# A selective-scan stage: diagonals by way of DRAM, and copies moved between VectorE and ScalarE

## The chip, the core and the metric

The kernel runs on one core of one Trainium2 chip. Its time is the device time of the whole program in microseconds (us). A core has a matrix engine (TensorE, "PE"; its weight loads are "PEld"), VectorE ("DVE"), ScalarE ("ACT"), GpSimd ("POOL") and SyncE ("SP", which here only issues transfers). The engines run side by side, each through its own instructions in program order, and wait for each other on counting semaphores.

## The reference, cut to what matters

The network is a convolutional state-space layer, then linear attention, then a spectral filter. The part at issue is the selective scan of the first layer. For each of 2 images and 4 directions `k` (rows, columns, and both backwards), with 256 channels, 16 states and 4096 positions:

```python
delta = softplus(dts + dt_proj_b)              # dts, B, C: projections of x
def step(h, inp):
    ut, dt, bt, ct = inp
    dA = exp(dt[..., None] * A)                # A = -exp(A_logs)
    h = dA * h + (dt * ut)[..., None] * bt     # one h for each channel and state
    y = einsum('bkdn,bkn->bkd', h, ct)
```

The four y are added in image order.

## The kernel before, in words

The program runs, for each image, a convolution, `scans`, and a norm with projection; then attention and the spectral filter for both. `scans` goes through 4 directions x 8 chunks of L = 512 positions, so 64 chunks in all. Channels lie on partitions in two halves t = 0, 1; positions lie along the free axis. Within a chunk (`body(c, nxt)`) all engines walk through the states n = 0..15:

- ScalarE: `decays(c, n, t)` (L617) makes exp(step x A). `times_b(c, n)` (L609) multiplies by B, which varies along positions: for even n it scales the turned x (position on partitions, `xu_tok`) into `scaled`; for odd n it scales the identity into four diagonal matrices `diag`. Both buffers are single, so `times_b(n)` waits until `drive(n-2)` is done (L605).
- PE: `drive(c, n)` (L508, L510) turns `scaled`, or multiplies `xu_tok` with `diag`, into `p_drive` in PSUM (two buffers, by the parity of n). It waits until scan n-2 has read the buffer. `sum_y` (L521) adds C x state into `p_y`.
- VectorE: `scan(c, n, t)` (L719) runs the recurrence over 512 positions; it needs `drive` and `decays` of that state and half. `state` is a ring of four.
- GpSimd: `times_c` (L663) multiplies the state by `c_wide`, and copies the last column to `carry` (L666), with which the next chunk starts.

While chunk c runs, the next one is prepared in the same loops: at n = 0 PE projects it (`project`), at n = 1 ScalarE copies that to `xd` (L582), at n = 3 and 4 PE makes the raw step of a half (`step_product`), at n = 4 and 5 VectorE takes its positive part (`step_bias`, L693, and L696 from the same function), at n = 6 and 7 ScalarE finishes the softplus (L593, L598), at n = 8 VectorE adds the two parts (`finish_step`, L701), GpSimd multiplies by u (`step_times_u`, L654), and PE turns the product (`turn_x`, L496, at n = 10 and 11), which VectorE copies to `xu_tok` (`keep_x`, L709). The y of the chunk before is copied from PSUM by VectorE after scan(3, 0) (`keep_y`, L726), turned back by PE and added by VectorE (`add_y`, L739). PE's order in a state n is: preparation, then `drive(n+2)`, then `sum_y(n-3)`. ScalarE's order is the loop

```python
for n in range(NS):
    of, at = following(c, nxt, n + 2)
    if of:
        decays(of, at, 0)
    of, at = following(c, nxt, n + 3)
    if of:
        times_b(of, at)
    of, at = following(c, nxt, n + 2)
    if of:
        decays(of, at, 1)
    if nxt and n in preparation:
        preparation[n](nxt)
```

and `decays(n, t)` waits for scan(n-2, t), for its buffer is double. SyncE stores the rows of C to DRAM (`store_c`) and loads them broadcast to all partitions, four states at a time (`widen_c`).

Of the kernel before, what the change touches and what calls it, by code (L numbers as in the profile page):

```python
# [9 lines left out]
fp32 = mybir.dt.float32  # L10
fp32r = mybir.dt.float32r
ALU = mybir.AluOpType
# [3 lines left out]
P = 128  # L16
# [7 lines left out]
NCH = T // L  # L24
START = 16
# [24 lines left out]
def constants(nc, m, io):  # L50


    with ExitStack() as ctx:
# [9 lines left out]
        w_conv = sb("w_conv", [P, 2, DT2, 9, P], fp32r)  # L63
        ps = [ctx.enter_context(nc.psum_tensor(f"wps{i}", [P, 512], fp32)) for i in range(8)]
# [30 lines left out]
        def _(pool):  # L95
# [12 lines left out]
                               pattern=[[4, 32], [0, 4]], channel_multiplier=-1).then_inc(made, 1)  # L108

# [89 lines left out]
def convolution(nc, m, io, b):  # L199


    with ExitStack() as ctx:
# [25 lines left out]
        def _(sp):  # L228
# [3 lines left out]
            sp.wait_ge(m.w_stored, 16)  # L232
# [121 lines left out]
    "projected", "xd_kept", "c_stored", "c_ready", "c_in0", "c_in1", "b_turned", "b_kept", "step_mm", "step_max",  # L354
# [38 lines left out]
def scans(nc, m, b):  # L393
# [3 lines left out]
    with ExitStack() as ctx:  # L397
        sb = lambda n, sh, d=fp32: ctx.enter_context(nc.sbuf_tensor(n, sh, d))
        ps = lambda n, sh: ctx.enter_context(nc.psum_tensor(n, sh, fp32))
        NB4 = L // P  # L400
# [7 lines left out]
        diag = sb("diag_b", [P, NB4, P])  # L408
# [24 lines left out]
        def _(sp):  # L433
            def store_c(c):
                sp.wait_ge(s["xd_kept"], START + c.g + 1)
                sp.dma_start(m.c_dram[c.parity], xd[C_ROW:C_ROW + NS, :]).then_inc(s["c_stored"], 16)
                sp.wait_ge(s["c_stored"], START + c.g * 16 + 16)
                sp.sem_inc(s["c_ready"], 1)
# [8 lines left out]
            def body(c, nxt):  # L447
                if c.first:
                    store_c(c)
                    widen_c(c, 0)  # L450
                    widen_c(c, 1)
# [10 lines left out]
        def _(pe):  # L462
# [37 lines left out]
            def drive(c, n):  # L500
                pe.wait_ge(s["scaled"], START + c.q + (n + 1))
                for t in range(DT2):
                    if not (c.first and n < 2):
                        pe.wait_ge(s["scanned"], START + c.q * 2 + (2 * n - 4 + t + 1))
                    for i in range(NB4):
# [3 lines left out]
                        else:  # L509
                            last = pe.matmul(o, xu_tok[:, c.parity, i, t * P:t * P + P], diag[:, i, :], start=True,  # L510
                                             stop=True)
# [64 lines left out]
        def _(act):  # L576
            def keep_projection(c):
# [3 lines left out]
                act.wait_ge(s["c_stored"], START + c.g * 16)  # L581
                act.copy(xd[:, :], p_prep[:, :]).then_inc(s["xd_kept"], 1)  # L582

            def keep_b(c):
                act.wait_ge(s["b_turned"], START + c.g + 1)
                rows = p_b[:, :].rearrange("p (i r) -> p i r", r=P)[:, :, B_ROW:B_ROW + NS]
                act.copy(b_tok[:, c.parity, :, :], rows).then_inc(s["b_kept"], 1)

# [11 lines left out]
            def times_b(c, n):  # L600
# [1343 lines left out]
```

## Time and profile before

| | |
|---|---|
| median of 3 runs | 6715.05 us (6708.61 to 6716.85) |
| the profiled execution | 6713.79 us, span 6712.1 us |
| busy, share of the span | PE 87%, PEld 77%, DVE 71%, ACT 52%, POOL 42% |
| mean granted TensorE clock | 0.954 |

A share is a mean over the whole span. The scans of the two images lie at about 180 to 1800 us and 2010 to 3640 us; from about 3700 us on the spectral filter runs, in which POOL is all but idle. A chunk is about 49 us, from one `finish_step` (L701) to the next.

### The profile page before, as it was taken

Reading aid. Unit: us, or ns where it says so; the run is one execution under the profiler, and the core shown is the slowest. Engines: PE = TensorE matmul, PEld = TensorE weight load, DVE = VectorE, ACT = ScalarE, POOL = GpSimd, SP = SyncE. Lnnn points to the kernel's source line nnn. Section 1 sums busy time; section 2 is a strip of 40 time slices with the busy share of each in tenths; the row PEclk is TensorE's granted clock in tenths of the full one; section 3 lists DMA queues with packets and bytes.
Section 4 is the critical chain, followed back from the end, with each engine's and each line's share of the span. In section 5 each row is a group of like instructions: output and inputs, shape, how many; then the busy total and the mean of one; then the engine's idle time right before and its main releaser. Section 6 shows DMA issues by size and latency. Waiting matters only on the chain. (4 is left out here: it accounts for less than half of the span.)

```text
span 6712.1 us, 130278 instructions
## 1 busy us (share of the span) xinstructions
PE 5830.3 (87%) x41691; PEld 5150.7 (77%) x41691; DVE 4764.7 (71%) x6882; ACT 3496.8 (52%) x7658; POOL 2798.1 (42%) x2159
## 2 busy tenths in 40 slices
PE   7789889898887998888888544999999989999998
PEld 6688778887766887888877333888888878888887
DVE  2799999999818999999997554555556556555554
ACT  2799999999737999999997211111111111111110
POOL 0688888888716888888887000000000000000000
PEclk8899999999988999999999877999999989999999
DMA  2122222222221222222222115666666667666665
GB/s 68 68 88 89 83 83 89 88 89 83 90 70 71 88 89 83 87 85 88 90 83 98 32 47 143 153 149 139 142 148 152 155 149 157 144 140 142 150 151 143
DMA packets 552406, 719.16 MB, mean 107 GB/s; under 512 B 37814, under 2 KB 458518, under 8 KB 518038
## 3 DMA queue, kind: packets, MB, share of 16 engines
q1 hardware_dynamic: 551382, 705.17, 38.6%
q10 hardware_dynamic: 720, 10.49, 0.4%
q8 instruction: 124, 2.03, 0.1%
q14 instruction: 180, 1.47, 0.1%
HBM read 677.22 MB, written 38.31 MB: 107 GB/s over the span
## 5 line engine op out<-in xcount | busy, mean ns | idle before, releaser
L663 POOL TENSOR_TENSOR read<-state,c_wide 128x1024 f32<-128x1024 f32 x1024 | 2435.0, 2378 | 459.2 <-DVE state L719 455.8
L719 DVE TENSOR_TENSOR_SCAN state<-decay,carry,p_drive 128x512 f32<-128x512 f32 x1792 | 2145.7, 1259 | 10.1 <-POOL carry L666 5.3
L617 ACT ACTIVATE decay<-step,a_neg 128x512 f32<-128x512 f32 x2048 | 1416.2, 714 | 230.2 <-DVE state L719 229.9
L1614 PE MATMUL p_y<-window,x_high 128*128 128x256 f32 x7936 | 1506.5, 288 | 0.0
L1677 ACT COPY term_blocks<-p_s 128x256 f32<-128x256 f32 x832 | 310.4, 373 | 2195.0 <-PE p_s L1614 2195.0
L1614 PEld LDWEIGHTS p_y<-window,x_high 128*128 128x128 f32 x7936 | 1253.9, 193 | 0.0
L510 PE MATMUL p_drive<-diag_b,xu_tok 128*128 128x128 f32 x8192 | 1101.3, 285 | 119.8 <-DVE state L719 116.1
L510 PEld LDWEIGHTS p_drive<-diag_b,xu_tok 128*128 128x128 f32 x8192 | 1007.8, 196 | 212.8 <-DVE state L719 151.2
L1614 PE MATMUL p_y<-window,x_low 128*128 128x256 f32 x3968 | 1138.8, 287 | 0.0
L521 PE MATMUL p_y<-ident,read 128*128 128x128 f32 x8192 | 1078.2, 275 | 3.8 <-POOL read L663 3.8
L521 PEld LDWEIGHTS p_y<-ident,read 128*128 128x128 f32 x8192 | 942.2, 143 | 4.7 <-POOL read L663 4.7
L609 ACT ACTIVATE scaled_x<-xu_tok,b_tok 128x256 f32<-128x256 f32 x2048 | 866.4, 494 | 44.7 <-DVE xu_tok L709 44.7
L1614 PEld LDWEIGHTS p_y<-window,x_low 128*128 128x128 f32 x3968 | 764.3, 193 | 0.0
L508 PE MATMUL p_drive<-ident,scaled_x 128*128 128x128 f32 x4096 | 574.8, 278 | 148.2 <-DVE state L719 136.4
L1614 PE MATMUL p_s<-window,x_high 128*128 128x256 f32 x2432 | 539.8, 310 | 148.3 <-DMA window<-taps_scratch 81.1
L508 PEld LDWEIGHTS p_drive<-ident,scaled_x 128*128 128x128 f32 x4096 | 462.3, 142 | 267.2 <-DVE state L719 175.0
L609 ACT ACTIVATE diag_b<-ident,b_tok 128x128 f32<-128x128 f32 x2048 | 648.6, 388 | 4.9 <-PE p_drive L510 4.5
L1614 PEld LDWEIGHTS p_s<-window,x_high 128*128 128x128 f32 x2432 | 390.2, 192 | 213.7 <-issue 118.7
L1734 DVE TENSOR_TENSOR term_blocks<-p_y,term_blocks 128x512 f32<-128x512 f32 x384 | 265.5, 692 | 354.2 <-PE p_y L1614 339.4
L1651 PE MATMUL p_mix<-term_blocks,mix_weights 128*128 128x512 f32 (+1 forms) x1280 | 461.2, 507 | 1.9 <-DVE term_blocks L1717 1.9
L1716 DVE TENSOR_TENSOR term_blocks<-p_y,term_blocks 128x256 f32<-128x256 f32 x448 | 187.7, 419 | 353.0 <-PE p_y L1614 352.1
L1651 PEld LDWEIGHTS p_mix<-term_blocks,mix_weights 128*128 128x128 f32 x1280 | 233.8, 190 | 152.0 <-issue 138.1
(245 smaller groups left out, 5822.3 us busy)
## 6 DMA issues: line engine op xcount, KB each, us to landing
c_wide<-c_scratch SPq DMA_DIRECT2D x256, 1024.0 KB, 4.6
window<-taps_scratch SPq DMA_DIRECT2D x448, 257.0 KB, 6.2
window<-taps_scratch SPq DMA_DIRECT2D x768, 129.0 KB, 4.6
window<-taps_scratch SPq DMA_DIRECT2D x192, 513.0 KB, 7.2
window<-taps_scratch SPq DMA_DIRECT2D x64, 385.0 KB, 5.9
gate_scratch<-gate_out SPq DMA_DIRECT2D x16, 512.0 KB, 3.1
gate_in<-gate_scratch SPq DMA_DIRECT2D x8, 1024.0 KB, 6.4
mix_weights<-in_M_plus SPq DMA_DIRECT2D x32, 256.0 KB, 7.2
```

Of the source, the lines that this page charges most:

```text
L508: last = pe.transpose(o, scaled[:, i, t * P:t * P + P], m.ident[:, :])
L510: last = pe.matmul(o, xu_tok[:, c.parity, i, t * P:t * P + P], diag[:, i, :], start=True, stop=True)
L521: last = pe.matmul(p_y[:, i, t * P:t * P + P], read[:, n % 4, t, i * P:i * P + P], m.ident[:, :], start=n == 0 and i % 2 == 0 and t == 0, ...
L609: last = act.activation(dst, src, ACT.Copy, scale=b_tok[:, c.parity, i, n:n + 1])
L617: act.activation(decay[:, n % 2, t, :], step[:, c.parity, t, :], ACT.Exp, scale=m.a_neg[:, DT2 * c.k + t, n:n + 1]).then_inc(s["decay"], 1)
L663: pool.tensor_tensor(read[:, n % 4, :, :], state[:, n % 4, :, :], wide, ALU.mult).then_inc(s["read_out"], 1)
L719: dve.tensor_tensor_scan(flip(state[:, n % 4, t, :], c), flip(decay[:, n % 2, t, :], c), flip(p_drive[:, n % 2, t, :], c), 0.0 if c.start ...
L1614: last = pe.matmul(out, x[:, source, blk, :], view[:, :, at:at + P][:, :, ::-1], start=first and x is m.x_high and z == 0, stop=True, skip ...
L1651: last = pe.matmul(p_mix[par][:, at:at + size], mix_now[:, kind, reach, :], filtered[:, j % 2, par ^ kind, kind, at:at + size], start=kind ...
L1677: act.copy(shared[:, i % 4, :, :], shared_bank(i)).then_inc(s["kept"], 1)
L1716: dve.tensor_tensor(to[:, :, 0:P], half_of(p_y[i % 4], 0), shared[:, i % 4, :, :], ALU.add)
L1734: dve.tensor_tensor(to.rearrange("p k (h t) -> p k h t", h=2), p_y[i % 4][:, :].rearrange("p (h k t) -> p k h t", h=2, k=2), out.rearrange ...
```

## The change

1. The diagonals of B for the 8 odd states are no longer made by ScalarE. SyncE writes the odd rows of B from `xd` into a zeroed DRAM scratch, each value to its place on a diagonal, and loads ready 128x128 matrices into `diag`, which now holds two groups of two odd states. The scratch is zeroed once at the start.
2. `keep_x` and `keep_y` become copies on ScalarE: at n = 10 and 11, and at the end of n = 3.
3. The positive part of the step becomes `step_max`, a Relu on ScalarE, at n = 4 and 5 between `times_b` and the second `decays`; VectorE keeps only `step_abs` there.
4. GpSimd copies the carries of two states at a time, after the odd one, and a scan of ring slot n waits for that pair.

```diff
@@ constants (sync) @@
+            sp.wait_ge(idmade, 4)
+            for parity in range(2):
+                sp.dma_start(m.diag_dram[parity].rearrange("(r x) -> r x", r=P), blank[:, :]).then_inc(m.w_stored, 16)
             sp.wait_ge(copied, 14)
@@ scans @@
-        diag = sb("diag_b", [P, NB4, P])
+        diag = sb("diag_b", [P, 2, 2, NB4, P])
@@ sync @@
-            def store_c(c):
+            def store_rows(c):
                 sp.wait_ge(s["xd_kept"], START + c.g + 1)
                 sp.dma_start(m.c_dram[c.parity], xd[C_ROW:C_ROW + NS, :]).then_inc(s["c_stored"], 16)
-                sp.wait_ge(s["c_stored"], START + c.g * 16 + 16)
-                sp.sem_inc(s["c_ready"], 1)
+                image = m.diag_dram[c.parity]
+                diagonals = bass.AP(tensor=image.tensor, offset=image.offset,
+                                    ap=[[NB4 * P * P, ODD], [P * P, NB4], [P + 1, P]])
+                rows = xd[B_ROW + 1:B_ROW + NS:2, :].rearrange("n (i p) -> n i p", p=P)
+                with nc.allow_non_contiguous_dma(reason="one value to each place of a diagonal"):
+                    sp.dma_start(diagonals, rows).then_inc(s["c_stored"], 16)
+
+            def load_diag(c, d):
+
+                if not (c.first and d < 2):
+                    sp.wait_ge(s["driven"], START + c.q * 2 + (8 * d - 8))
+                at = 2 * d * NB4 * P * P
+                src = m.diag_dram[c.parity, at:at + 2 * NB4 * P * P].rearrange("(n p q) -> p n q", n=2 * NB4, p=P)
+                sp.dma_start(diag[:, d % 2, :, :, :].rearrange("p n i q -> p (n i) q"), src).then_inc(
+                    s[f"diag_in{d % 2}"], 16)
...
+                load_diag(c, 2)
+                if nxt:
+                    store_rows(nxt)
                 widen_c(c, 2)
+                load_diag(c, 3)
                 widen_c(c, 3)
                 if nxt:
-                    store_c(nxt)
+                    sp.wait_ge(s["c_stored"], START + nxt.g * 32 + 32)
+                    load_diag(nxt, 0)
                     widen_c(nxt, 0)
+                    load_diag(nxt, 1)
                     widen_c(nxt, 1)
@@ tensor: drive @@
-                pe.wait_ge(s["scaled"], START + c.q + (n + 1))
+                if n % 2 == 0:
+                    pe.wait_ge(s["scaled"], START + c.g * ODD + (n // 2 + 1))
+                elif n % 4 == 1:
+                    pe.wait_ge(s[f"diag_in{n // 4 % 2}"], START + c.g * 32 + (16 * (n // 8) + 16))
@@ scalar @@
+            def step_max(c, t):
+                act.wait_ge(s["step_mm"], START + c.g * 2 + (t + 1))
...
+                act.activation(step[:, c.parity, t, :], p_prep[:, :], ACT.Relu, bias=bias).then_inc(s["step_max"], 1)
...
                 for i in range(NB4):
-                    dst, src = ((scaled[:, i, :], xu_tok[:, c.parity, i, :]) if n % 2 == 0 else
-                                (diag[:, i, :], m.ident[:, :]))
-                    last = act.activation(dst, src, ACT.Copy, scale=b_tok[:, c.parity, i, n:n + 1])
+                    last = act.activation(scaled[:, i, :], xu_tok[:, c.parity, i, :], ACT.Copy,
+                                          scale=b_tok[:, c.parity, i, n:n + 1])
...
+            def keep_y(c):
+                act.wait_ge(s["summed"], START + c.q + NS)
+                act.wait_ge(s["y_turned"], START + c.g * 2)
+                act.copy(y_tok[:, :, :], p_y[:, :, :]).then_inc(s["y_kept"], 1)
...
-                    if of:
+                    if of and at % 2 == 0:
                         times_b(of, at)
+                    if nxt and n in (4, 5):
+                        step_max(nxt, n - 4)
                     of, at = following(c, nxt, n + 2)
                     if of:
                         decays(of, at, 1)
+                    if n == 3 and not c.first:
+                        keep_y(Before(c))
                     if nxt and n in preparation:
                         preparation[n](nxt)
+                    if nxt and n in (10, 11):
+                        keep_x(nxt, n - 10)
@@ gpsimd @@
-                pool.tensor_copy(carry[:, n, :], state[:, n % 4, :, end]).then_inc(s["carried"], 1)
+                if n % 2:
+                    pool.tensor_copy(carry[:, n - 1:n + 1, :], state[:, n % 4 - 1:n % 4 + 1, :, end]).then_inc(s["carried"], 1)
@@ vector @@
-            def step_bias(c, t):
+            def step_abs(c, t):
+                dve.wait_ge(s["step_max"], START + c.g * 2 + (t + 1))
...
-                dve.tensor_scalar(step[:, c.parity, t, :], p_prep[:, :], bias, 0.0, ALU.add,
-                                  ALU.max).then_inc(s["step_max"], 1)
-                dve.wait_ge(s["step_max"], START + c.g * 2 + (t + 1))
                 dve.scalar_tensor_tensor(softplus[:, t, :], step[:, c.parity, t, :], -2.0, p_prep[:, :], ALU.mult,
                                          ALU.add).then_inc(s["step_abs"], 1)
...
-                        dve.wait_ge(s["carried"], START + c.q + (n - 3))
+                        dve.wait_ge(s["carried"], START + c.g * ODD + (n // 2 - 1))
...
                 for n in range(NS):
                     scan(c, n, 0)
-                    if n == 3 and not c.first:
-                        keep_y(Before(c))
                     if n in (6, 7) and not c.first:
                         add_y(Before(c), n - 6)
                     if nxt and n in (4, 5):
-                        step_bias(nxt, n - 4)
+                        step_abs(nxt, n - 4)
                     if nxt and n == 8:
                         finish_step(nxt)
-                    if nxt and n in (11, 12):
-                        keep_x(nxt, n - 11)
                     scan(c, n, 1)
```

## Rows read from the trace of the kernel before

**Rows 1.** Windows by stage; columns: engines' busy us, granted clock, DMA share, GB/s.

```profile
300.00:1500.00 1200.00, 1075.39 (x8479) 968.33 (x8480) 1108.04 (x1024) 1108.05 (x2460) 1030.11 (x804) 0.99 0.23 87
...
3700.00:6712.00 3012.00, 2622.06 (x17944) 2332.23 (x17944) 1698.70 (x4027) 414.50 (x974) 0.84 (x5) 0.94 0.59 136
```

**Rows 2.** Timeline of VectorE, one chunk: start, duration, what, idle before.

```profile
891.71 1.39 DVE L701 TENSOR_TENSOR step<-step,shared 128x1024 f32<-128x1024 f32 x1 [1.05 <-ACT shared L598]
...
903.65 16.50 DVE L719 TENSOR_TENSOR_SCAN state<-decay,carry,p_drive 128x512 f32<-128x512 f32 x14
922.05 1.23 DVE L726 COPY y_tok<-p_y 128x1024 f32<-128x1024 f32 x1 [1.90 <-PE p_y L521]
...
926.31 0.69 DVE L696 SCALAR_TENSOR_TENSOR shared<-step,p_prep 128x512 f32<-128x512 f32 x1
...
930.04 0.69 DVE L696 SCALAR_TENSOR_TENSOR shared<-step,p_prep 128x512 f32<-128x512 f32 x1
930.65 2.44 DVE L719 TENSOR_TENSOR_SCAN state<-decay,carry,p_drive 128x512 f32<-128x512 f32 x2
...
941.26 1.40 DVE L701 TENSOR_TENSOR step<-step,shared 128x1024 f32<-128x1024 f32 x1 [1.04 <-ACT shared L598]
```

**Rows 3.** Timeline of PE over the same chunk.

```profile
899.41 0.66 PE L496 MATMUL p_prep<-ident,shared 128*128 128x128 f32 x4 [0.69 <-POOL shared L654]
...
920.00 1.04 PE L508 MATMUL p_drive<-ident,scaled_x 128*128 128x128 f32 x8
920.87 1.04 PE L521 MATMUL p_y<-ident,read 128*128 128x128 f32 x8
```

**Rows 4.** Timeline of ScalarE over the same chunk.

```profile
922.89 1.69 ACT L609 ACTIVATE scaled_x<-xu_tok,b_tok 128x256 f32<-128x256 f32 x4
924.50 0.72 ACT L617 ACTIVATE decay<-step,a_neg 128x512 f32<-128x512 f32 x1
```

**Rows 5.** Timeline of GpSimd over the same chunk.

```profile
896.84 0.20 POOL L666 COPY carry<-state 128x2 f32<-128x2 f32 x1
896.98 2.37 POOL L654 TENSOR_TENSOR shared<-step,s 128x1024 f32<-128x1024 f32 x1
```

**Rows 6.** Groups, 180 to 3640 us: busy us, mean ns, idle before.

```profile
L663 POOL TENSOR_TENSOR read<-state,c_wide 128x1024 f32<-128x1024 f32 x1024 | 2435.0, 2378 | 459.2 <-DVE state L719 455.8 <-PE p_y L521 3.0
...
L617 ACT ACTIVATE decay<-step,a_neg 128x512 f32<-128x512 f32 x2048 | 1416.2, 714 | 230.2 <-DVE state L719 229.9
...
L609 ACT ACTIVATE scaled_x<-xu_tok,b_tok 128x256 f32<-128x256 f32 x2048 | 866.4, 494 | 44.7 <-DVE xu_tok L709 44.7
L609 ACT ACTIVATE diag_b<-ident,b_tok 128x128 f32<-128x128 f32 x2048 | 648.6, 388 | 4.9 <-PE p_drive L510 4.5
...
L693 DVE TENSOR_SCALAR step<-p_prep,dt_b 128x512 f32<-128x512 f32 x128 | 93.0, 727 | 261.1 <-PE p_prep L485 261.1
...
L709 DVE COPY xu_tok<-p_prep 128x512 f32<-128x512 f32 x128 | 86.9, 679 | 24.7 <-PE p_prep L496 23.9 <-ACT diag_b L609 0.8
L593 ACT ACTIVATE shared<-shared,dt_b 128x512 f32<-128x512 f32 x128 | 84.6, 709 | 14.1 <-DVE shared L696 14.1
...
L726 DVE COPY y_tok<-p_y 128x1024 f32<-128x1024 f32 x64 | 78.4, 1225 | 122.5 <-PE p_y L521 122.5
...
L582 ACT COPY xd<-p_prep 128x512 f32<-128x512 f32 x64 | 36.2, 566 | 5.9 <-PE p_prep L467 5.9
```

**Rows 7.** Timeline of SyncE at the start.

```profile
26.82 0.34 SPq L91 DMA_DIRECT2D w_conv_scratch<-w_conv  x1
```

**Rows 8.** Timeline of ScalarE, two places before the scans.

```profile
9.94 0.31 ACT L113 ACTIVATE a_neg<-a_neg 128x128 f32<-128x128 f32 x1 [7.84 <-DMA b_qkv<-in_attn_b]
...
181.61 1.28 ACT L620 ACT_TABLE_LOAD   x1 [3.78 <-PEq L202]
```

**Rows 9.** DMA issues: count, KB each, median us to landing.

```profile
c_wide<-c_scratch SPq DMA_DIRECT2D x256, 1024.0 KB, 4.6
...
c_scratch<-xd SPq DMA_DIRECT2D x64, 32.0 KB, 4.3
```

More of the change, by code:

```diff
@@ L24 @@
 NCH = T // L
+NB4 = L // P
+ODD = NS // 2
 START = 16
@@ L108, in _ @@
                                pattern=[[4, 32], [0, 4]], channel_multiplier=-1).then_inc(made, 1)
+            pool.memset(blank[:, :], 0.0).then_inc(idmade, 1)
         @block.scalar
@@ L509, in drive @@
                         else:
-                            last = pe.matmul(o, xu_tok[:, c.parity, i, t * P:t * P + P], diag[:, i, :], start=True,
-                                             stop=True)
+                            last = pe.matmul(o, xu_tok[:, c.parity, i, t * P:t * P + P],
+                                             diag[:, n // 4 % 2, n // 2 % 2, i, :], start=True, stop=True)
                     last.then_inc(s["driven"], 1)
@@ L587, in keep_b @@
                 act.copy(b_tok[:, c.parity, :, :], rows).then_inc(s["b_kept"], 1)
+            def step_max(c, t):
+                act.wait_ge(s["step_mm"], START + c.g * 2 + (t + 1))
+                if t == 0 and not c.first:
+                    act.wait_ge(s["decay"], START + c.q * 2 + -2 * NS)
+                bias = m.dt_b[:, DT2 * c.k + t:DT2 * c.k + t + 1]
+                act.activation(step[:, c.parity, t, :], p_prep[:, :], ACT.Relu, bias=bias).then_inc(s["step_max"], 1)
             def step_exp(c):
@@ L618, in decays, with keep_x @@
                                scale=m.a_neg[:, DT2 * c.k + t, n:n + 1]).then_inc(s["decay"], 1)
+            def keep_x(c, half):
+                act.wait_ge(s["x_turned"], START + c.g * 2 + (half + 1))
+                if not c.first:
+                    act.wait_ge(s["scaled"], START + c.g * ODD + -ODD)
+                    act.wait_ge(s["driven"], START + c.q * 2 + -2 * NS)
+                act.copy(xu_tok[:, c.parity, 2 * half:2 * half + 2, :],
+                         p_prep[:, :].rearrange("p (i d) -> p i d", d=DI)).then_inc(s["x_kept"], 1)
+            def keep_y(c):
+                act.wait_ge(s["summed"], START + c.q + NS)
+                act.wait_ge(s["y_turned"], START + c.g * 2)
+                act.copy(y_tok[:, :, :], p_y[:, :, :]).then_inc(s["y_kept"], 1)
             act.preload_act_table_set("natural_log_exp_and_others")
@@ L626, in body @@
                     keep_b(c)
+                    step_max(c, 0)
+                    step_max(c, 1)
                     step_exp(c)
                     step_ln(c)
-                    for n in range(2):
-                        times_b(c, n)
+                    keep_x(c, 0)
+                    keep_x(c, 1)
+                    times_b(c, 0)
                     for n in range(2):
@@ L644, in body @@
                         decays(of, at, 1)
+                    if n == 3 and not c.first:
+                        keep_y(Before(c))
                     if nxt and n in preparation:
                         preparation[n](nxt)
+                    if nxt and n in (10, 11):
+                        keep_x(nxt, n - 10)
+                if c.last:
+                    keep_y(c)
             chunk_stream(act, b, body)
@@ L684, in begin_y @@
                                          ALU.mult, ALU.add).then_inc(s["y_begun"], 1)
-            def step_bias(c, t):
-                dve.wait_ge(s["step_mm"], START + c.g * 2 + (t + 1))
+            def step_abs(c, t):
+                dve.wait_ge(s["step_max"], START + c.g * 2 + (t + 1))
                 if t == 0:
                     dve.wait_ge(s["x_turned"], START + c.g * 2)
-                    if not c.first:
-                        dve.wait_ge(s["decay"], START + c.q * 2 + -2 * NS)
-                bias = m.dt_b[:, DT2 * c.k + t:DT2 * c.k + t + 1]
-                dve.tensor_scalar(step[:, c.parity, t, :], p_prep[:, :], bias, 0.0, ALU.add,
-                                  ALU.max).then_inc(s["step_max"], 1)
-                dve.wait_ge(s["step_max"], START + c.g * 2 + (t + 1))
                 dve.scalar_tensor_tensor(softplus[:, t, :], step[:, c.parity, t, :], -2.0, p_prep[:, :], ALU.mult,
@@ L742, in body @@
                 if c.first:
-                    step_bias(c, 0)
-                    step_bias(c, 1)
+                    step_abs(c, 0)
+                    step_abs(c, 1)
                     begin_y(0)
```

28 lines of the change are left out of this document (9 added, 19 removed).

## The prediction

> **What bounds the kernel now.** I read the stages first [rows 1]: in a stretch of scans PE, VectorE, ScalarE and GpSimd are all busy for 1030 to 1108 of 1200 us, while the spectral stage is 3012 us that the change does not touch. So only some 3250 us of scans are at stake, in 64 chunks, and there no engine is far ahead of the rest: what matters is which wait ends last. The shares of the whole span hide that.
>
> Next I took one ordinary chunk, from `finish_step` at 891.71 to the next at 941.26, 49.55 us [rows 2], and looked at each engine in it. VectorE runs 14 scans in 16.50 us, 1.18 each, and after scan(3, 0) waits 1.90 us for PE's last sum before `keep_y`. Why is PE late? It starts `turn_x` at 899.41 after waiting for GpSimd's product, and from there has no idle row until `drive(4)` at 920.00 and the sum behind it at 920.87 [rows 3]. So from n = 10 to n = 3 PE sets the pace; VectorE, with its two x copies, only fits beside it. From `keep_y` to the next `finish_step` it is VectorE's turn: its operations follow each other, and PE, GpSimd and ScalarE wait for scans. That ScalarE does is seen in the groups: the decays wait 229.9 us, all for scans [rows 6]. The chunk is thus a loop of two parts, and each has to be priced by itself.
>
> **The change part by part.** *x copies.* VectorE gives up 128 copies of 679 ns [rows 6]. They lie in the part that PE paces, so I price the gain at nothing; without that cover it would be 2 x 0.6 x 64 = 77 us. *Diagonals on ScalarE.* 2048 activations of 388 ns go [rows 6], 648.6 us of busy time, but they were not what anyone waited for in either part, save that ScalarE's backlog vanishes: it reached `times_b(6)` at 922.89 [rows 4], though `drive(4)` was over at 920.00 + 1.04 = 921.04. PE's odd drives are the same matmuls. *Carries.* The product by u started 0.14 us after the carry before it [rows 5]. With n = 8 no longer copied it and the whole PE part come 0.15 us earlier. The pair makes an even scan wait for GpSimd's state n-3 instead of n-4. GpSimd needs at most 2.378 a state [rows 6] plus 0.14 a pair, 4.9, against 4.72 for four scans; nearly a tie, and the PE part covers it.
>
> *The second part, from `drive(4)` on,* is where the sign is decided. Before, `drive(4)` starts at 920.00 and scan(5, 1) at 930.65 [rows 2, 3], 10.65 us. Now it holds ScalarE's in-order list, so I write it out. An operation costs its mean less the 0.08 by which the next overlaps it (924.50 against 922.89 + 1.69 [rows 4]), except where another engine waits for its end. Prices [rows 6]: a decay 0.63; `times_b` 1.61; Relu with a bias column as the exponential with one, 0.71 (L593; a plain copy of that size, L582, is 0.57 and is the lower bound); the y copy 0.99, from the copy of 512 (0.566) and 0.106 for each further 128 elements (0.494 less 0.388), so 0.91 to the next start.
>
> - `drive(4)` starts at 919.85, ends at 920.9. ScalarE, with keep_projection behind it, is there about 921.0: `times_b(6)` to 922.6, second decay of state 5 to 923.25, `keep_y` (the sum is done by 921.8) to 924.15, first decay of state 6 to 924.8, `step_max` to 925.5.
> - Meanwhile scan(4, 0) has ended before 923, and VectorE stands at `step_abs(0)` until 925.55. It takes 0.61 (930.65 less 930.04 [rows 2]), so scan(4, 1) starts at 926.15. Before, `step_abs(0)` started at 926.31 [rows 2], so its scan at 926.92: 0.8 us gained here.
> - scan(4, 1) and scan(5, 0) end at 926.15 + 2.44 = 928.6. Only then may ScalarE start the decay of state 7 (it reads the buffer's release from scan(5, 0)): to 929.25, then `times_b(8)`, which stands ahead of `step_max(1)` because 5 + 3 is even: to 930.85, then Relu to 931.55. `step_abs(1)` from 931.6, scan(5, 1) at 932.2 against 930.65.
>
> So VectorE is spared 1.14 for y and twice 0.76, and stands still some 3 us at each of two places instead: net 1.5 us a chunk later. From scan(5, 1) on all is as before: the softplus is reached after the decays of state 8, so the wait of 1.04 before `finish_step` stays [rows 2]. Queued behind ScalarE's `keep_y` are just those decays and the Relu; PE's `sum_y(0)` waits for it too, but PE has the next `step_product` and `drive(5)` first. Behind VectorE's wait stands every scan.
>
> Bounds: with both Relus at 0.57, their ends overlapped and ScalarE free at 920.9, 0.9 a chunk; with ScalarE's backlog or the carry pairs adding 0.4, 1.9. Sixty chunks have both neighbours: 60 x 1.5 = 90 us (54 to 114). First and last chunks of an image have only one of the two parts; a few us either way, taken as 0.
>
> *The DRAM way.* 4096 values of 4 bytes are written and 2 MB of matrices loaded each chunk. The stretch of scans uses 0.23 of the DMA engines [rows 1]; a load of 1024 KB lands in 4.6 us, so four of 512 KB in at most that each, and the store of C in 4.3 [rows 9]. Scattered stores of single values are not in the trace. Nearest is the start: thirteen weight loads, several of single values, have landed by 9.94 us [rows 8]. I bound the store by 4.3 us below and 20 above (twice the whole start). It is issued about two states before `keep_y`, near 917, and its matrices are needed for `drive(1)`, some seven states after the next `finish_step`, near 958: less 5 for the load there are 36 us of cover, so it costs nothing. The C rows queued behind it on SyncE's queue have four states' notice, and `times_c` now waits only for scans (L663 [rows 6]). If cover failed, each us beyond would cost 60.
>
> The Trainium skill (DMA: Bandwidth & Descriptors, Rules for kernel authors) says that a non-contiguous last dimension becomes one descriptor per element, and (Why a DMA increments its semaphore by 16 and not by 1) that the slowest dimension limits the engines used; here it is 8, so this store would take 8 of 16 engines. No row here shows that; by it the store is slower than one spread over 16, which leaves the sum alone unless 36 us are passed.
>
> *Start.* 4 MB of zeros are stored before the w_conv store at 26.82 [rows 7]. Queued behind the loads that landed at 9.94 [rows 8] at 4.6 us a MB they end near 28.3, so 0 to 2 us. First chunks: `store_rows` is covered by the long additions of y.
>
> The Relu on ScalarE costs 0.71 where VectorE took 0.727 [rows 6], about equal by itself. The Trainium skill (ScalarE: Activation LUTs, Rules for kernel authors) says to use VectorE, not ScalarE, for relu. The trace agrees with no large difference in duration; it is the place in the list that hurts, which that rule does not price.
>
> The profiled execution took 6713.8, 1.3 below the median. 6713.8 + 90 + 1 = 6805. A difference within 0.2% (13 us) can hardly be told from none.
>
> **The rivals.**
>
> *VectorE relieved (faster), 0.18.* If ScalarE answered in time, the y copy with its wait (1.90 + 1.14) and two Relus (1.52) would go, 4.55 a chunk, less about 1.1 because `step_product(0)` comes only after the sum: 3.4 x 60 = 205, 6510. For it: VectorE is the busiest in the scans with ScalarE [rows 1], and 258 us of its busy time go [rows 6]. Against: the written order. It decides where `drive(4)` to scan(5, 1) takes under 10.8 us; I have 12.3. An in-between, PE reaching `drive(4)` a us or two sooner, gives 6650 to 6700.
>
> *A draw, 0.05:* the gain at `step_abs(0)` is larger (the sum earlier, copies shorter) and meets the loss at `step_abs(1)`. 6715.
>
> *The scattered store is late, 0.05:* at 50 us instead of under 36, each chunk is 14 longer: 7550. For it: its price is unknown. It then shows as PE waiting for a DMA before an odd `drive`.
>
> *Relu needs its table, 0.02:* a load takes 1.28 us [rows 8]; two Relus between exponentials need four, 5.1 us a chunk, 7020 or more. Against: copy, exponential and logarithm already alternate without a load.
>
> **How the numbers follow.** The likeliest case, 0.70, is slower by 50 to 120 us: its own range is 6765 to 6835, its centre 6805. With the draw that is 0.75; reaching down to 6650 takes in the mild third of the faster case, 0.05 to 0.06, and up to 6850 an overshoot of my own. Slower 0.70 + 0.05 + 0.02 = 0.77, same 0.05, faster 0.18.
>
> **What would show it.** In the chunk's timeline after: VectorE idle 2.5 to 3 us before each of the two `step_abs`, released by ScalarE's Relu; no idle before the y copy's old place; 12.3 us from `drive(4)` to scan(5, 1); a chunk of some 51 us; VectorE's busy time 258 us less and its share lower, not higher. ScalarE's rows in order: decay, `times_b`, Relu. I am wrong if those two waits are under 2 us each, if `drive(4)` lies well before 28 us after `finish_step`, or if PE waits for a matrix load.

## The result and the profile after

The changed kernel takes 6788.58 us (median of four runs, 6785.8 to 6799.3) against 6714.93 before on the same chip (6708.61 to 6716.85): ratio 1.0111, interval 1.0094 to 1.0127. The change makes the kernel slower by 1.1%, some 74 us. The forecast was 6805 us, with a range of 6650 to 6850.

The page of the changed kernel, head and busy time:

```profile
span 6788.2 us, 128900 instructions
...
PE 5829.7 (86%) x41691; PEld 5188.8 (76%) x41691; DVE 4552.1 (67%) x6562; ACT 3123.5 (46%) x5930; POOL 2735.6 (40%) x1648
```

The window that answers to [rows 1], a stretch in the scans (engines' busy us with counts, in the order PE, weight loads, VectorE, ScalarE, GpSimd; then granted clock, DMA share, GB/s):

```profile
300.00:1500.00 1200.00, 1047.61 (x8273) 955.67 (x8271) 1002.09 (x880) 942.99 (x1763) 980.51 (x595) 0.97 0.48 126
```

Every engine is less busy in the same 1200 us and none has become the bound: they wait for each other more. The DMA engines' share has doubled, from 0.23 to 0.48, with the matrices and the scattered store. Who waits is in the groups from 180 to 3700 us (busy us, mean ns, idle before and its releasers); VectorE:

```profile
L753 DVE SCALAR_TENSOR_TENSOR shared<-step,p_prep 128x512 f32<-128x512 f32 x128 | 88.0, 688 | 644.5 <-ACT step L626 644.5
L758 DVE TENSOR_TENSOR step<-step,shared 128x1024 f32<-128x1024 f32 x64 | 82.4, 1288 | 87.3 <-ACT shared L637 87.3
```

ScalarE:

```profile
L655 ACT ACTIVATE decay<-step,a_neg 128x512 f32<-128x512 f32 x2044 | 1422.0, 717 | 600.1 <-DVE state L768 589.1
L646 ACT ACTIVATE scaled_x<-xu_tok,b_tok 128x256 f32<-128x256 f32 x2048 | 867.5, 495 | 53.9 <-PE p_drive L540 53.6
L626 ACT ACTIVATE step<-p_prep,dt_b 128x512 f32<-128x512 f32 x128 | 85.8, 671 | 9.5 <-PE p_prep L514 9.5
...
L663 ACT COPY xu_tok<-p_prep 128x512 f32<-128x512 f32 x128 | 73.9, 577 | 78.9 <-PE p_prep L525 78.9
...
L669 ACT COPY y_tok<-p_y 128x1024 f32<-128x1024 f32 x63 | 62.5, 993 | 8.1 <-PE p_y L553 8.1
```

`step_abs` (L753) waits 644.5 us for ScalarE's Relu. Two waits, 256.6 of these, stand at the first chunk of each image, where 256.3 of the 261.1 before L693 in [rows 6] stood too; the other 388 are new. ScalarE itself is idle more than before, 600.1 us against 230.2 ahead of the decays, and nearly all of it for VectorE's scans. The two engines wait for each other in turn; neither is short of time.

One ordinary chunk shows it. VectorE, from one `finish_step` (L758) to the next, answering to [rows 2]:

```profile
913.54 1.39 DVE L758 TENSOR_TENSOR step<-step,shared 128x1024 f32<-128x1024 f32 x1 [1.05 <-ACT shared L637]
914.86 8.30 DVE L768 TENSOR_TENSOR_SCAN state<-decay,carry,p_drive 128x512 f32<-128x512 f32 x7
923.53 14.39 DVE L768 TENSOR_TENSOR_SCAN state<-decay,carry,p_drive 128x512 f32<-128x512 f32 x12 [0.38 <-POOL carry L729]
938.48 5.97 DVE L768 TENSOR_TENSOR_SCAN state<-decay,carry,p_drive 128x512 f32<-128x512 f32 x5 [0.56 <-PE p_drive L540]
947.81 0.69 DVE L753 SCALAR_TENSOR_TENSOR shared<-step,p_prep 128x512 f32<-128x512 f32 x1 [3.36 <-ACT step L626]
948.41 2.44 DVE L768 TENSOR_TENSOR_SCAN state<-decay,carry,p_drive 128x512 f32<-128x512 f32 x2
953.82 0.69 DVE L753 SCALAR_TENSOR_TENSOR shared<-step,p_prep 128x512 f32<-128x512 f32 x1 [2.96 <-ACT step L626]
954.43 2.45 DVE L768 TENSOR_TENSOR_SCAN state<-decay,carry,p_drive 128x512 f32<-128x512 f32 x2
...
965.04 1.41 DVE L758 TENSOR_TENSOR step<-step,shared 128x1024 f32<-128x1024 f32 x1 [1.04 <-ACT shared L637]
```

ScalarE between `drive(4)` and the second Relu of that chunk:

```profile
943.29 1.70 ACT L646 ACTIVATE scaled_x<-xu_tok,b_tok 128x256 f32<-128x256 f32 x4
944.88 0.71 ACT L655 ACTIVATE decay<-step,a_neg 128x512 f32<-128x512 f32 x1
945.50 0.99 ACT L669 COPY y_tok<-p_y 128x1024 f32<-128x1024 f32 x1
946.39 0.73 ACT L655 ACTIVATE decay<-step,a_neg 128x512 f32<-128x512 f32 x1
947.01 0.67 ACT L626 ACTIVATE step<-p_prep,dt_b 128x512 f32<-128x512 f32 x1
949.72 0.72 ACT L655 ACTIVATE decay<-step,a_neg 128x512 f32<-128x512 f32 x1 [2.04 <-DVE state L768]
950.89 0.72 ACT L655 ACTIVATE decay<-step,a_neg 128x512 f32<-128x512 f32 x1 [0.45 <-DVE state L768]
951.52 1.69 ACT L646 ACTIVATE scaled_x<-xu_tok,b_tok 128x256 f32<-128x256 f32 x4
953.12 0.67 ACT L626 ACTIVATE step<-p_prep,dt_b 128x512 f32<-128x512 f32 x1
```

and PE's `drive(4)`, from whose start the forecast counts the second part:

```profile
942.08 1.04 PE L540 MATMUL p_drive<-ident,scaled_x 128*128 128x128 f32 x8
```

The wait of 2.96 us is made by VectorE itself: it stands at `step_abs` for a Relu that stands behind a decay (950.89) that had to wait for VectorE's scan. The list adds 0.72 + 1.69 + 0.67 before it lets VectorE go. Over the 62 intervals of the table below the two waits are 3.19 and 2.97 us on the mean; before, both were 0.03.

Over all 62 intervals from one `finish_step` to the next inside an image, mean start times behind `finish_step`, in us (my tabulation of the two timelines):

| | `turn_x` | `drive(4)` | first `step_abs` | second `step_abs` | next `finish_step` |
|---|---|---|---|---|---|
| before | 8.01 | 28.40 | 34.67 | 38.39 | 49.29 |
| after | 7.87 | 27.95 | 33.68 | 39.69 | 50.62 |

A chunk is 1.33 us longer: 62 x 1.33 = 82 us. The first `finish_step` is 2.1 later (203.7 to 205.9), the gap between the images 1.6 shorter, and all that follows the last `finish_step`, nearly only stages that the change does not touch, 6.4 shorter: 76 in all, as the spans have it (6788.2 less 6712.1). These last three differences are no larger than the scatter between the profiles: in those of the experiments the first `finish_step` lies between 200.7 and 205.4 us, and what follows the last takes 3141 to 3170.

The matrices come in time (count, KB each, median us to landing, answering to [rows 9]):

```profile
c_wide<-c_scratch SPq DMA_DIRECT2D x256, 1024.0 KB, 4.8
diag_b<-diag_scratch SPq DMA_DIRECT2D x256, 512.0 KB, 4.0
```

PE has no wait for a DMA in any group of the scans.

### The profile page after: what moved, and what is told of

It is laid out like the page before. It is cut to its first block and busy times, and to the rows that moved or that the text cites. A ratio compares the mean times of both kernels' runs of the same rounds, so it can differ in the third digit from the quotient of the medians.

```text
span 6788.2 us, 128900 instructions
## 1 busy us (share of the span) xinstructions
PE 5829.7 (86%) x41691; PEld 5188.8 (76%) x41691; DVE 4552.1 (67%) x6562; ACT 3123.5 (46%) x5930; POOL 2735.6 (40%) x1648
## 2 busy tenths in 40 slices
DMA packets 1081526, 858.12 MB, mean 126 GB/s; under 512 B 304598, under 2 KB 987446, under 8 KB 1046966
## 5 line engine op out<-in xcount | busy, mean ns | idle before, releaser
L542 PE MATMUL p_drive<-diag_b,xu_tok 128*128 128x128 f32 x8192 | 1087.7, 286 | 200.6 <-DVE state L768 200.6
L553 PE MATMUL p_y<-ident,read 128*128 128x128 f32 x8192 | 1097.8, 279 | 6.9 <-POOL read L725 3.7
L553 PEld LDWEIGHTS p_y<-ident,read 128*128 128x128 f32 x8192 | 962.6, 145 | 8.2 <-POOL read L725 8.2
L540 PEld LDWEIGHTS p_drive<-ident,scaled_x 128*128 128x128 f32 x4096 | 477.9, 145 | 227.1 <-DVE state L768 142.0
L753 DVE SCALAR_TENSOR_TENSOR shared<-step,p_prep 128x512 f32<-128x512 f32 x128 | 88.0, 688 | 644.5 <-ACT step L626 644.5
```

What stands on the lines that cost most here:

```text
L540: last = pe.transpose(o, scaled[:, i, t * P:t * P + P], m.ident[:, :])
L553: last = pe.matmul(p_y[:, i, t * P:t * P + P], read[:, n % 4, t, i * P:i * P + P], m.ident[:, :], start=n == 0 and i % 2 == 0 and t == 0, ...
```

## The experiments

Times are medians; a ratio is to the kernel before, run on the same chip. A difference in us is worked out from a ratio: its distance from 1, times 6715. Chips differ by some us (the kernel before took 6708 to 6733), so an expected time is compared with 6715 times the ratio.

**1. The changed kernel with the positive part back on VectorE.** The rest of the change stays.

```
-                dve.wait_ge(s["step_max"], START + c.g * 2 + (t + 1))
+                dve.wait_ge(s["step_mm"], START + c.g * 2 + (t + 1))
...
+                dve.tensor_scalar(step[:, c.parity, t, :], p_prep[:, :], bias, 0.0, ALU.add,
+                                  ALU.max).then_inc(s["step_max"], 1)
```

> The changed kernel with one part undone: the positive part of the step is again made by VectorE, in front of step_abs. Theory (the loss is the Relu behind other work in ScalarE's list): in the changed kernel's chunk VectorE would start scan(4, 1) near 946.45 instead of 948.41 and scan(5, 1) near 950.3 instead of 954.43, so about 4.2 us a chunk less than the changed kernel, 6788.6 - 62 x 4.2 = 6530 (6490 to 6600), well faster than before; VectorE's idle time before step_abs falls from 644 us to under 300. Rival (the diagonals' transfers, or the pair copies of the carries, cost the time): it stays at 6715 or above.

6567.85 us, ratio 0.9762 (0.9744 to 0.978), inside what was expected. A chunk falls to 46.81. The Relu's move alone decides the sign: with it 1.1% slower, without it 2.4% faster, 234 us apart.

**2. The changed kernel with the Relu at the head of its state in ScalarE's list,** ahead of the decays and `times_b`; same engine, same instruction.

```
                 for n in range(NS):
+                    if nxt and n in (4, 5):
+                        step_max(nxt, n - 4)
                     of, at = following(c, nxt, n + 2)
```

> The changed kernel with step_max moved to the head of its state in ScalarE's list, ahead of both decays and of times_b; nothing else differs. Theory (the place in the list): the second Relu is ready when scan(5, 0) ends, scan(5, 1) starts near 950.85 instead of 954.43, 3.6 us a chunk: 6788.6 - 62 x 3.6 = 6565 (6520 to 6640). Rival (ScalarE is the wrong engine for a Relu whatever its place, or handing over between engines costs the time): no more than 1 us a chunk, 6725 or above.

6601.42 us, ratio 0.9806 (0.9787 to 0.9825). The second wait is all but gone and the first shorter (0.20 and 2.63 us on the mean):

```profile
946.53 0.69 DVE L753 SCALAR_TENSOR_TENSOR shared<-step,p_prep 128x512 f32<-128x512 f32 x1 [2.52 <-ACT step L626]
947.13 2.44 DVE L768 TENSOR_TENSOR_SCAN state<-decay,carry,p_drive 128x512 f32<-128x512 f32 x2
949.77 0.69 DVE L753 SCALAR_TENSOR_TENSOR shared<-step,p_prep 128x512 f32<-128x512 f32 x1 [0.20 <-ACT step L626]
```

So 0.0305 of the ratio, 205 of the 234 us, goes with the place in the list, the engine being the same. That is the step on which the forecast's sign stood.

**3. The Relu alone moved to ScalarE,** in the kernel before.

> The kernel before with one part done: the positive part of the step as a Relu on ScalarE at the place that the change gives it. Here times_b is there for odd states too, so it stands ahead of both Relus. Theory: step_abs(0) starts about 1.9 us later than before and step_abs(1) another 2.2, 4.1 us a chunk: 6715 + 62 x 4.1 = 6970 (6900 to 7020). Rival (the Relu costs nothing by itself, the loss comes from the other parts): within 20 us of 6715.

7029.53 us, ratio 1.0444 (1.0423 to 1.0465): 298 us slower, in the upper end of what was expected (7013 by the ratio), and a chunk is 54.15. VectorE has its y copy with the wait for the sum, and the two waits for the Relu besides:

```profile
937.23 1.23 DVE L731 COPY y_tok<-p_y 128x1024 f32<-128x1024 f32 x1 [2.00 <-PE p_y L521]
938.37 2.44 DVE L724 TENSOR_TENSOR_SCAN state<-decay,carry,p_drive 128x512 f32<-128x512 f32 x2
943.43 0.69 DVE L701 SCALAR_TENSOR_TENSOR shared<-step,p_prep 128x512 f32<-128x512 f32 x1 [2.62 <-ACT step L594]
944.03 2.44 DVE L724 TENSOR_TENSOR_SCAN state<-decay,carry,p_drive 128x512 f32<-128x512 f32 x2
949.43 0.69 DVE L701 SCALAR_TENSOR_TENSOR shared<-step,p_prep 128x512 f32<-128x512 f32 x1 [2.96 <-ACT step L594]
```

The mechanism is the same; together with the other parts of the change it costs less.

**4. The y copy alone on ScalarE.**

```
-                dve.tensor_copy(y_tok[:, :, :], p_y[:, :, :]).then_inc(s["y_kept"], 1)
+                act.copy(y_tok[:, :, :], p_y[:, :, :]).then_inc(s["y_kept"], 1)
```

> The kernel before with one part done: the copy of y on ScalarE at the end of n = 3. Theory (the y copy is where the change gains): scan(5, 1) starts about 1.2 us sooner, then ScalarE's odd times_b make up the rest: 6715 - 74 = 6640 (6600 to 6690). Rival (the y copy on ScalarE delays decays and costs as well): 6715 or above.

6701.9 us, ratio 0.9956 (0.994 to 0.9972): 30 us gained, where some 75 were expected. VectorE no longer waits for the sum, but for the raw step (`step_product`), which PE makes behind it. The profile names a decay before the first of the two, but PE ends the first raw step at 917.83:

```profile
918.19 0.75 DVE L702 TENSOR_SCALAR step<-p_prep,dt_b 128x512 f32<-128x512 f32 x1 [0.82 <-ACT decay L617]
...
923.37 0.75 DVE L702 TENSOR_SCALAR step<-p_prep,dt_b 128x512 f32<-128x512 f32 x1 [1.35 <-PE p_prep L485]
```

The group before `step_bias` is idle 393.4 us against 261.1 in [rows 6], 132 in 62 intervals or 2.1 a chunk, and PE's sums wait 69.2 us for the later `y_tok`. Of the 3.1 us freed (1.90 + 1.23 [rows 2]) most went there.

**5 to 7. The other parts alone,** in the kernel before: the diagonals by way of DRAM; the two x copies on ScalarE; one carry copy for two states.

> The kernel before with one part done: the diagonals of B by way of DRAM, all else as before (positive part, x copies and y copy on VectorE, a carry copy for each state). Theory (the transfers lie under 36 us of cover, and ScalarE's diagonals were not waited for, save a backlog of some tenths): PE reaches drive(4) up to 0.3 us a chunk sooner, 6715 - 19, so 0 to 30 us less than the kernel before on this chip. Rival (the transfers contend with the engines or come late): 13 us or more above it.

> The kernel before with one part done: the two x copies of a chunk on ScalarE. Theory (they lie in the part of the chunk that PE paces, where VectorE has slack): no gain from VectorE's 1.3 us a chunk; ScalarE, which here still makes the odd diagonals, gets 1.0 us a chunk more in that part, so 0 to 40 us above the kernel before. Rival (VectorE's load sets the time of this part): 1.2 us a chunk less, about 75 us below it.

> The kernel before with one part done: the carries copied in pairs. Theory (nearly a tie, covered by PE; only the copy at n = 8 shortens the way to PE's turn_x by 0.14 us): 0 to 10 us below the kernel before. Rival (the scan's wait for a younger state costs): VectorE's idle time before even scans of 0.4 us and more a chunk reaches PE's drives, 25 us or more above it.

The diagonals: 6751.98, ratio 1.0032 (1.0022 to 1.0043), 21 us slower where a draw or a small gain was expected: a miss. The x copies: 6771.91, 1.006 (1.0046 to 1.0073), 40 slower, the upper end of what was expected. The pairs: 6722.97, 0.9989 (0.998 to 0.9998), 7 faster, as expected.

Why do the x copies cost 40 us alone? Their groups on VectorE:

```profile
L723 DVE TENSOR_TENSOR_SCAN state<-decay,carry,p_drive 128x512 f32<-128x512 f32 x1792 | 2164.4, 1262 | 84.7 <-ACT decay L617 39.5 <-PE p_drive L508 29.0 <-PE p_drive L510 9.9
L723 DVE TENSOR_TENSOR_SCAN state<-decay,p_drive 128x512 f32<-128x512 f32 x256 | 295.1, 1202 | 36.0 <-ACT decay L617 28.6 <-PE p_drive L508 5.4 <-PE p_drive L510 1.6
```

The scans wait 68.1 us for decays, against 8.0 in the kernel before. From `turn_x` to `drive(4)` a chunk takes 20.97 us and not 20.39. With `times_b` for all sixteen states, ScalarE seems to have no room for two copies between n = 10 and n = 3.

**8. The best kernel: experiment 1 with the logarithm directly behind the exponential,** at n = 6 and not 7.

```
-            preparation = {1: keep_projection, 6: step_exp, 7: step_ln, 9: keep_b}
+            preparation = {1: keep_projection, 6: lambda c: (step_exp(c), step_ln(c)), 9: keep_b}
```

> The version with the positive part on VectorE again (6568 us), and ScalarE's logarithm directly behind its exponentials at n = 6, ahead of times_b for state 10. Theory (the second part of a chunk is VectorE's chain, and the wait of 1.05 us before finish_step is all ScalarE's order): that wait goes, 62 x 1.05 = 65 less: 6503 (6490 to 6530). Rival (PE or GpSimd sets the chunk by now): no more than 20 us less, 6548 or above.

6546.91 us, ratio 0.9727 (0.9712 to 0.9742): faster than both kernels, but only some 23 us under experiment 1, where 65 were expected: a miss. `finish_step` no longer waits for ScalarE; it takes twice as long instead. VectorE, then GpSimd over the same stretch:

```profile
943.57 2.53 DVE L760 TENSOR_TENSOR step<-step,shared 128x1024 f32<-128x1024 f32 x1
```

```profile
942.65 2.37 POOL L721 TENSOR_TENSOR read<-state,c_wide 128x1024 f32<-128x1024 f32 x1 [1.18 <-DVE state L770]
944.96 1.18 POOL L725 COPY carry<-state 128x4 f32<-128x4 f32 x1
```

GpSimd's product ends at 945.02. `finish_step`, 1.29 us long in the changed kernel's group, ends at 946.10, 1.1 behind that, as if it had begun only then; and GpSimd's carry, 0.20 elsewhere, ends at 946.14, at the same time as it. In all 62 intervals inside an image `finish_step` starts before the product's end and ends 1.08 or 1.09 us behind it. From experiment 1 to this one, 64 `finish_step` go from 1298 to 2525 ns, 79 us, and the 88.9 us of waiting before them, which went, are thus nearly all paid back. The Trainium skill (SBUF — State Buffer, SBUF: two separate sides) says that a VectorE operation with two inputs in SBUF and a GpSimd operation that reads SBUF exclude each other, and whoever comes second is fully held up. `finish_step` has two such inputs, and the trace agrees, in both directions. What was expected of this run did not reckon with it.

**9. All but the diagonals:** the four other parts together, while ScalarE still makes the diagonals.

> The whole change except its first part: the kernel before with the positive part, the copy of summed y and the copies of turned x on ScalarE and the carries in pairs, while ScalarE still makes the diagonals of B for the odd states. If the parts simply add up, the time is that of the kernel before plus what each of the four did alone (297 for the positive part, -30 for y, +40 for x, -7 for the pairs), about 300 more: 7015 (6960 to 7070), and the diagonals by way of DRAM, which cost 21 alone, are worth some 225 in company. If ScalarE's list can't be shortened by the DRAM way at the places that matter, the four parts together cost little more than the whole change did: 6790 (6760 to 6830). If a list without slack makes each delay feed the next, it is above 7070.

7070.55 us, ratio 1.0523 (1.0506 to 1.0539): 351 us slower, 50 more than the four parts one by one, so each delay feeds the next a little; it is just inside the range expected for a plain sum (7066 by the ratio, where the range ended at 7070). VectorE's first wait is 6.34 us (6.33 on the mean):

```profile
1007.27 0.69 DVE L723 SCALAR_TENSOR_TENSOR shared<-step,p_prep 128x512 f32<-128x512 f32 x1 [6.34 <-ACT step L594]
```

and ScalarE's list, idle nowhere, says why:

```profile
1001.60 1.69 ACT L616 ACTIVATE scaled_x<-xu_tok,b_tok 128x256 f32<-128x256 f32 x4
1003.19 0.70 ACT L624 ACTIVATE decay<-step,a_neg 128x512 f32<-128x512 f32 x1
1003.80 0.99 ACT L630 COPY y_tok<-p_y 128x1024 f32<-128x1024 f32 x1
1004.70 0.72 ACT L624 ACTIVATE decay<-step,a_neg 128x512 f32<-128x512 f32 x1
1005.32 1.26 ACT L616 ACTIVATE diag_b<-ident,b_tok 128x128 f32<-128x128 f32 x4
1006.49 0.66 ACT L594 ACTIVATE step<-p_prep,dt_b 128x512 f32<-128x512 f32 x1
```

ScalarE comes late to `times_b(6)`, 3.0 us behind the start of `drive(4)` (998.56) and not 1.2, and `times_b(7)` stands before the Relu too. The diagonals' way through DRAM, a loss of 21 us alone, is worth 0.0523 less 0.0111, 277 us, within the change.

**10. The best kernel with the x copies back on VectorE.**

> The quickest kernel so far (changed kernel, positive part back on VectorE, logarithm directly behind the exponential) with the copies of turned x back on VectorE as well, directly ahead of the second scans at n=11 and 12. If the copies on ScalarE are covered, as the prediction had it, VectorE's two copies of about 0.7 us each are pure addition where VectorE sets the pace and nothing where PE sets it: 0 to 60 slower than the same kernel with them on ScalarE, 6547 to 6610. If they stand in ScalarE's way there, as alone (+40), moving them back gains: 6505 to 6547.

6575.16 us, ratio 0.979 (0.9775 to 0.9806): 42 us slower than experiment 8. Here the copies on ScalarE are a gain, where alone they were a loss of 40. The gain lies in the part that PE was said to pace: from `turn_x` to `drive(4)` a chunk takes 20.74 us with them on VectorE and 20.18 with them on ScalarE.

**11 and 12. What the diagonals cost alone.** Experiment 5 without the scattered store; then also with each later load cut from 512 to 4 KB. In both the images stay zero, so the odd states' input is left out.

```
-                    sp.dma_start(diagonals, rows).then_inc(s["c_stored"], 16)
...
+                    row = m.diag_dram[c.parity, at:at + 2 * NB4 * P].rearrange("(p q) -> p q", p=1)
+                    sp.dma_start(diag[0:1, d % 2, :, :, :].rearrange("p n i q -> p (n i q)"), row).then_inc(
```

> The diagonals' part alone once more, without the store of the 4-byte values: the images in DRAM stay zero, so that the odd states' input is left out (their products with zero are still computed), and the four loads of 512 KB a chunk remain. If the 20 us that the part cost alone come from the scattered store (its 5.5 us on the DMA engines), the time is that of the kernel before or a little less: ratio 0.997 to 1.000, and the eight chunks that were 2 to 4.7 us longer are of the common length. If they come from the loads, which occupy the DMA engines for much longer, the ratio stays at 1.002 to 1.004 and the eight chunks stay long.

> The diagonals' part alone, without the store of the 4-byte values and with each later load of 512 KB cut to one row of 4 KB that reads the same zeros, so that every wait and semaphore stays and the odd states' input is left out. The run before it, with the loads whole, was 1.0046 of the kernel before, and five chunk intervals in it were 51 to 55 us against 49.2. If the loads' traffic on the DMA engines is the cause (it delays something else that comes by DMA, such as the engines' code at a change of loop), the ratio falls to 0.997 to 1.001 and no chunk interval is above 51 us except those that the kernel before has too. If the cause lies in the instructions themselves (the new order of PE's waits, ScalarE's shorter list), the ratio stays at 1.003 to 1.006 with the same long chunks.

Without the store 6749.73, ratio 1.0046 (1.0033 to 1.0059): nothing gained. With the small loads 6714.45, ratio 1.0011 (1.0002 to 1.002); one of its twelve executions took 11642 us, for a reason that nothing here shows, and the ratio leaves it out. So the loads cost the 20 us or so, and the store nothing. They cost it in eight chunks, the fourth and sixth of the first and of the last direction in each image: these chunks start with a jump back of the loop over chunks (`chunk_stream`). One of them reads, without the store and with full loads:

```profile
359.16 7.11 DVE L746 TENSOR_TENSOR_SCAN state<-decay,carry,p_drive 128x512 f32<-128x512 f32 x6
370.16 8.31 DVE L746 TENSOR_TENSOR_SCAN state<-decay,carry,p_drive 128x512 f32<-128x512 f32 x7 [3.89 <-issue]
```

VectorE stands 3.89 us before the chunk's first scan though its inputs are there ("issue": it waits for nothing that the profile shows). Before four of the eight the profile names GpSimd's carry of state 15 instead, for which by the code this scan does not wait. The eight idle times add up to 10.0 us in the kernel before, 32.2 with the diagonals alone, 31.2 without the store, 16.6 with the small loads, and 0.0 in the changed kernel. The 21.2 us from the kernel before to experiment 11 are nearly all of the 24.5 that its chunk intervals are longer.

What VectorE stands for can be read from the DMA packets. The page of a profile lists, beside the data queues, DMA queues of kind "instruction"; their name says that they bring code. In experiments 5, 11 and 12 these idle times last from 1.5 to 4.6 us, but each ends a fixed time behind the end of an 8 KB packet of that kind: 2.06 to 2.17 us in the first direction, 1.28 to 1.50 in the last (my reading of the packets). With full loads that packet ends 0.6 to 3.2 us after the idle time begins, with small ones between 0.6 before and 1.3 after. By these times it is code that VectorE waits for, though no packet names its engine. That the packets come later because they stand behind the loads on the DMA engines is likely, and not shown.

## Why the prediction was right

**The second part, which carried the sum, came out as written.** From the start of `drive(4)`, forecast and measured in the chunk shown: `times_b(6)` 1.15 and 1.21, first decay 2.75 and 2.80, Relu 4.95 and 4.93, first `step_abs` 5.70 and 5.73, second 11.75 and 11.74, scan(5, 1) 12.35 and 12.35. On the mean, 9.99 became 11.74 to the second `step_abs`, 1.75 more. The forecast's times give 1.7 for it, 1.55 later in the chunk and 0.15 by the earlier `drive(4)`; its sum took 1.5 for the 1.55. From there on nothing changed: 10.90 and 10.93 to the next `finish_step`.

**The first part gave more than forecast.** `drive(4)` came 0.45 us sooner, not 0.15: 0.14 before `turn_x`, as forecast, and 0.31 between it and `drive(4)`. So 1.5 a chunk was 1.33: 0.1 more in the second part, 0.3 less in the first; the two errors partly cancel, and the 0.3 is the size that was off. There are 62 such intervals and not 60, so the 90 us were 82. The term behind it is most likely the x copies, priced at nothing because PE was said to pace this part: 40 us lost alone (experiment 6), and 42 gained where the positive part is on VectorE and the diagonals come from DRAM, 0.56 of it a chunk between `turn_x` and `drive(4)` (experiment 10). No run takes them out of the changed kernel itself.

**The diagonals at nothing was right for the wrong neighbours.** In the kernel before nobody waited for them, and taking them away gives no time (experiment 12: 1.0011). But they are what would have stood in the Relu's way: without that part the kernel is 351 us slower than before and not 74 (experiment 9). The forecast treated the list as it would be after the whole change, so its sum holds; it never said what this part was worth. That the loads delay VectorE's code at some loop turns, which it did not foresee, did it no harm either: those waits are absent from the changed kernel, and why they are is open.

**The DRAM way is covered.** SyncE's queue waited for the store twice, 7.1 us each, at the images' first chunks, and PE never for a matrix. From its issue to its last completion the store takes 10.0 us in the median chunk, between the forecast's bounds of 4.3 and 20. Its 4-byte packets ran from about 944.6 to 950.1 us of the chunk shown. In the middle of it nothing else moves; the window (columns as above):

```profile
946.00:948.00 2.00, 1.89 (x18) 1.65 (x16) 0.19 (x1) 1.69 (x3) 1.45 (x2) 1.00 0.90 3
```

These are 3 GB/s, and yet the packets' times add up to 0.90 of sixteen engines' time. A `c_wide` load queued behind it landed in 8.4 us and not 4.8, unnoticed by anyone. Both rules of the Trainium skill (DMA: Bandwidth & Descriptors) agree with the trace. One descriptor per element (Rules for kernel authors): the profile after has 1081526 packets against 552406 before; 64 stores of 4096 values are 262144 of the 529120 more, and the matrices' loads nearly all the rest. That the slowest dimension, 8 here, limits the engines used (Why a DMA increments its semaphore by 16 and not by 1): each scattered store brings nine updates of its semaphore, one 1.1 us after its issue and eight at its end, while the store of C and each load of C or of matrices bring sixteen (my count of the updates). By the same section of the Trainium skill each engine used reports its own end, and the issuing sequencer reports for the others at once; read so, the trace shows 8 engines. The share of 0.90 is no sign against it, for packets can overlap on an engine: up to 25 packets of 512 bytes are under way at once in this trace. Neither rule touched the sum.

**Pairs, start and busy time.** `turn_x` came 0.14 us sooner, as forecast for the pair; with the pair alone it came 0.05 sooner, and the kernel was 7 us faster (experiment 7). The start took 2.1 us more, just above the forecast's 0 to 2, but within the scatter between profiles. VectorE's busy time fell by 213 us (4764.7 to 4552.1) and not by 258: the forecast added up durations, although most operations overlap the next by some 0.08 us, which accounts for about half of the difference. The first of the two waits, 3.19 us on the mean, is over the forecast's 2.5 to 3.

**The Relu on ScalarE** takes 671 ns and not 710, against 727 on VectorE. It is worth 234 us to have it back on VectorE (experiment 1), and 205 us come already by moving it up in ScalarE's own list (experiment 2). The Trainium skill (ScalarE: Activation LUTs, Rules for kernel authors) says to keep relu on VectorE; that is right here, but for the place and not for the duration.

**The rivals.** "VectorE relieved" failed at the place named: 12.3 us, not under 10.8. Experiments 1 and 2 show that it was one list entry away. The late store, the table load (34 loads in both profiles) and the draw did not happen.

## What to carry to other kernels

Before work moves to another engine, write out that engine's list around the new entry: what stands ahead of it, and whether any of that waits for the engine it is meant to relieve. If so, the two take turns, and the move costs more than its duration, however idle both are. And price the parts together: here five parts that cost 322 us one by one (298 - 30 + 40 + 21 - 7) cost 74 as a whole, since one of them makes the room that the others use.

## What the runs showed of the hardware

A VectorE operation with two inputs in SBUF grew from 1298 to 2525 ns where it met GpSimd's product, and GpSimd's carry of 0.20 us to 1.18 behind it: a wait removed from one engine's list can come back inside the instruction, where no idle time shows it. One DMA of 4096 single values took 10.0 us from issue to its end, with eight completions of sixteen, and cost nothing measurable (experiment 11 against 5). Loads that raise the DMA engines' share from 0.23 to 0.38 (experiment 11) lengthened VectorE's idle time at eight turns of a loop, from 0.6 to 2.0 us each to 2.6 to 4.6, and the profile names no cause or a wrong one; each of these waits ends a fixed time behind a packet of code. The Trainium skill (Runtime: NRT & Kernel Launch, Instruction fetch mechanics) says that an engine's code comes by DMA and that a taken branch outside the window forces a fetch. The packets agree with it by their times; that the branch is what forces this fetch, no run here shows.
